# Filler products in TensorE's planned waits, k ahead of q, and another table of urgencies in a one-core decoder layer

## The reference

```python
# 1: causal self-attention, rotated before a second projection
q, k, v = rope(x @ wq.T), rope(x @ wk.T), x @ wv.T   # v is rotated too
qh, kh, vh = q @ wqi.T + bqi, k @ wki.T + bki, v @ wvi.T + bvi
x = layernorm(x + softmax(causal(qh @ kh.T / sqrt(8))) @ vh @ out_w.T + out_b)
# 2: cross-attention to the context, rotary on q and k
x = layernorm(x + attention(rope(x @ Wq.T + bq), rope(ctx @ Wk.T + bk), ctx @ Wv.T + bv) @ Wo.T + bo)
# 3: mixture of experts, the two best of eight by x @ wg.T
x = layernorm(x + sum_e weight_e * ((silu(x @ w1[e].T) * (x @ w3[e].T)) @ w2[e].T))
```

## Time and profile before

| | us |
|---|---|
| Median of 3 runs (259.11 to 260.6) | 259.66 |
| The profiled execution, its time | 258.49 |
| Its span, first to last instruction | 256.7 |

### The profile page before, as it was taken

One profiled execution on the slowest core, in us unless ns is written; L12 is line 12 of the kernel. 1 busy time (PEld: TensorE's weight loads), 2 busy tenths in 40 slices (PEclk: granted clock), 3 DMA queues, 4 the chain that ended last, 5 costly groups with the idle time before them and its releaser, 6 DMA issues. The chain is left out here.

```text
span 256.7 us, 4503 instructions
## 1 busy us (share of the span) xinstructions
PE 233.5 (91%) x1385; PEld 161.8 (63%) x1385; DVE 183.8 (72%) x616; ACT 158.4 (62%) x315; POOL 93.9 (37%) x151
## 2 busy tenths in 40 slices
PE   7679899999999999999998886999799998999980
PEld 3247556677665765586554365655378896898870
DVE  6558987888999697784847468694166884189855
ACT  1677857687898866886787642456656666122140
POOL 9993436165416164332535501065000100730100
PEclk9988999999999999999999997699999999999997
DMA  6980000011000400000221100001401111110101
GB/s 240 339 291 0 4 0 1 0 51 35 3 0 0 166 1 0 4 0 0 77 87 44 43 1 0 0 33 52 127 28 43 42 43 31 43 38 3 42 1 41
DMA packets 10567, 12.55 MB, mean 49 GB/s; under 512 B 1200, under 2 KB 7728, under 8 KB 10416
## 3 DMA queue, kind: packets, MB, share of 16 engines
q1 hardware_dynamic: 9456, 10.43, 12.6%
q0 software_dynamic: 512, 1.05, 1.4%
q10 hardware_dynamic: 576, 0.79, 0.9%
HBM read 9.25 MB, written 3.01 MB: 48 GB/s over the span
## 5 line engine op out<-in xcount | busy, mean ns | idle before, releaser
L1500 DVE CUSTOM_DVE_ANT_0 junk<-psA,c 128x128 bf16<-128x128 f32 (+3 forms) x128 | 55.9, 487 | 10.2 <-PE psA L1002 9.7
L1286 ACT ACTIVATE prob<-psB 128x512 f32<-128x512 f32 (+1 forms) x88 | 47.6, 560 | 14.6 <-PE psB L1031 11.6
L1031 PE MATMUL psB<-qb,kst 128*128 128x512 f32 (+3 forms) x128 | 38.6, 345 | 0.9 <-ACT prob L1286 0.6
L1002 PE MATMUL psA<-kst,qa 128*128 128x512 f32 (+1 forms) x88 | 36.8, 436 | 1.8 <-ACT kst L1249 1.4
L1505 DVE TENSOR_REDUCE negm<-psA 128x3 f32<-128x462 f32 (+1 forms) x48 | 26.0, 577 | 9.6 <-PE psA L1002 9.3
L1031 PEld LDWEIGHTS psB<-qb,kst 128*128 128x128 f32 x128 | 22.8, 188 | 14.8 <-ACT prob L1286 5.7
L1286 ACT ACTIVATE prob_more<-psB 128x512 f32<-128x512 f32 (+1 forms) x48 | 25.0, 527 | 7.8 <-PE psB L1031 7.4
L854 POOL TENSOR_SCALAR_AFFINE_SELECT prob<-prob 128x256 f32<-128x256 f32 x32 | 13.1, 408 | 40.2 <-ACT prob_more L1286 40.1
L1328 ACT ACTIVATE silu<-psA 128x512 f32<-128x512 f32 x16 | 9.5, 597 | 24.1 <-DVE hid L1661 14.2
L1002 PEld LDWEIGHTS psA<-kst,qa 128*128 128x128 f32 x88 | 16.8, 194 | 9.8 <-issue 6.0
L1002 PE MATMUL psA<-kc,qa 128*128 128x462 f32 (+2 forms) x64 | 19.3, 358 | 1.9 <-DVE negm L1505 1.9
(11 more groups left out here) (190 smaller groups left out, 541.9 us busy)
## 6 DMA issues: line engine op xcount, KB each, us to landing
c<-w_dram SPq DMA_DIRECT2D x8, 256.0 KB, 2.6
w<-w_dram SPq DMA_DIRECT2D x1, 1024.0 KB, 4.7
xs_dram<-kst SPq DMA_DIRECT2D x1, 960.0 KB, 7.2
ys_dram<-ys SPq DMA_DIRECT2D x7, 128.0 KB, 1.8
rest<-xs_dram SPq DMA_DIRECT2D x3, 256.0 KB, 2.7
c<-c_dram SPq DMA_DIRECT2D x1, 666.0 KB, 8.5
xT<-xt_dram SPq DMA_DIRECT2D x2, 256.0 KB, 4.8
x_tok<-x_dram SPq DMA_DIRECT2D x1, 512.0 KB, 10.0
```

The lines of the kernel that those rows point to most:

```text
L1002: last = nc.tensor.matmul(ps[:, c:c + heads * width].rearrange("p (n w) -> p n w", n=heads), qa[:, u % SLOTS, 128 * i:128 * i + 128], keys ...
L1031: last = nc.tensor.matmul(ps[:, c:c + S - 128 * kt], keys, qb[:, u % 2, 128 * kt:S], start=m == 0, stop=m == len(blocks) - 1, skip_group_c ...
L1286: nc.scalar.activation(dst, psB[n % SIZE["B"]][:, 0:cols], ACT.Exp, scale=SCALE).then_inc(b_done[n % SIZE["B"]], 1)
L1500: last = nc.vector.tensor_tensor_reduce(out=junk[:, p, cols], in0=psA[p][:, cols], in1=c32[:, C_MASK + S - width:C_MASK + S], scale=-1.0, ...
```

## The change

Three things change together.

- k takes the first place of q in each batch: U, H and the parts go k, q, v. PART and the buffer numbers derived from it follow, and so do the bias columns.
- A function `fillers()` goes over the planned order of PE in two stretches: from the second item to the first B of unit 0, and from the last B of units before 12 to the first B of unit 12 (cross-attention of batch 1). Where an item that ends after 6 us is planned to begin over 0.45 us after the end of the one before it, PE makes int((gap - 0.15) / 0.14) products ahead of it whose result nobody reads: in the first stretch zeros by 320 columns of the warm-up tile into psO; in the second, constants of c16 by 256 columns into the bank of psB that the next B will overwrite.
- The table EARLY is replaced as a whole.

```diff
-ROPE = {(b, w): "DVE" if (b, w) in ((0, "q"), (0, "k")) else "POOL" for b in range(B) for w in "qkv"}
+ROPE = {(b, w): "DVE" if (b, w) in ((0, "q"), (0, "k")) else "POOL" for b in range(B) for w in "kqv"}
...
-PART = {("q", 0): 0, ("k", 0): 1, ("q", 1): 2, ("k", 1): 3, ("c",): 4, ("x", 0): 5, ("x", 1): 6}
+PART = {("k", 0): 0, ("q", 0): 1, ("k", 1): 2, ("q", 1): 3, ("c",): 4, ("x", 0): 5, ("x", 1): 6}
...
-        for n, w in enumerate("qkv"):
+        for n, w in enumerate("kqv"):
...
-                before = (("H", (m // 3, "qk"[m % 3])) if m % 3 < 2 else ("VH", (m // 3,)), 0)
+                before = (("H", (m // 3, "kq"[m % 3])) if m % 3 < 2 else ("VH", (m // 3,)), 0)
...
-                deps.append((("H", (0, "k")), 0))
+                deps.append((("H", (0, "q")), 0))
...
-        for w in "qk":
+        for w in "kq":
...
 EARLY = {
-    ('A', 11): -36, ('A', 14): -9, ('A', 3): 80, ('A', 5): -7, ('A', 8): 65, ('A', 9): -52, ('B', 0): -26, ('B', 10): 139,
-    ('B', 11): 8, ('B', 12): 6, ('B', 5): 107, ('CV',): -8, ('F1', 1): -10, ('F1', 14): -29, ('F2', 0): -16, ('F2', 4): -9,
-    ('F3', 1): -3, ('F3', 9): -15, ('LN', 2, 0): -44, ('MP', 9): 13, ('MT', 1): -63, ('MT', 2): 28, ('MT', 4): -30,
-    ('MT', 9): -75, ('ONT', 0, 1): -45, ('OP', 0, 0): -52, ('OP', 0, 1): 67, ('OP', 1, 1): -73, ('OT', 7): -57,
...
-    ('SQ', 0, 1, 0): -24, ('SQ', 1, 0, 0): -27, ('U', 1, 'k'): -28, ('U', 1, 'v'): -42, ('VH', 0): 27, ('XS', 3): -75,
+    ('A', 10): -26, ('A', 11): -53, ('A', 15): -4, ('A', 3): -3, ('A', 6): -4, ('A', 7): -46, ('A', 8): 52, ('A', 9): -104,
+    ('B', 0): -81, ('B', 11): -22, ('B', 12): 4, ('B', 5): 133, ('CK',): 18, ('F1', 14): -50, ('F2', 0): -7, ('F2', 4): -31,
+    ('F3', 1): -12, ('F3', 3): -10, ('F3', 7): -3, ('F3', 9): -28, ('LN', 2, 0): -69, ('MP', 13): 18, ('MT', 11): -17,
+    ('MT', 2): 41, ('MT', 9): -115, ('ONT', 0, 0): -16, ('ONT', 0, 1): -65, ('OP', 0, 0): -44, ('OT', 2): -33,
+    ('OT', 7): -99, ('PV', 1): -51, ('PV', 12): -75, ('PV', 8): -22, ('PV', 9): -12, ('R1', 3): -2, ('R1', 4): -19,
...
+    ('SK', 1, 0): -11, ('SQ', 0, 0, 1): -25, ('SQ', 0, 1, 2): 11, ('U', 1, 'q'): -39, ('U', 1, 'v'): -64, ('XS', 1): 9,
 }
...
+def fillers():
+
+    table = tasks()
+    order = ORDER["PE"]
+    first, last = order.index(("B", (0, 0))), order.index(("B", (B * NG + NG, 0)))
+    hole = max(n for n, item in enumerate(order) if item[0] == "B" and item[1][0] < B * NG + NG and n < last)
+    counts = {}
+    for n in [*range(1, first), *range(hole + 1, last)]:
+        item, before = order[n], order[n - 1]
+        if item == before:
+            continue
+        gap = ENDS[item, 0] - table[item][0][0][1] - ENDS[before, 0]
+
+        if ENDS[item, 0] > 6 and gap > 0.45:
+            counts[item] = int((gap - 0.15) / 0.14)
+    return counts
+
+
+FILLERS = fillers()
...
-            for item in ORDER["PE"]:
+            for n_item, item in enumerate(ORDER["PE"]):
                 kind, args = item
+                if item in FILLERS:
+                    ahead = [other for other in ORDER["PE"][n_item:] if other[0] == "B"][0]
+                    ps = psO
+                    if ahead[1][0]:
+
+                        loaded(s_c16, 16)
+                        ps = ring_bank("B", ahead)
+                    for _ in range(FILLERS[item]):
+                        if ahead[1][0]:
+                            nc.tensor.matmul(ps[:, 0:256], c16[:, 0:128], c16[:, 0:256], start=True, stop=True)
+                        else:
+                            nc.tensor.matmul(ps[:, 0:320], warm[:, 384:512], warm[:, 0:320], start=True, stop=True)
...
-    bcol = [ib[0:D], ib[D:2 * D], bq, bq[swap4], bk, bk[swap4]]
+    bcol = [ib[D:2 * D], ib[0:D], bq, bq[swap4], bk, bk[swap4]]
```

More of the change, by code:

```diff
@@ L709, in parts_made @@
                 b, w = divmod(n, 2)
-                job_done(eng, "H", b, "qk"[w])
+                job_done(eng, "H", b, "kq"[w])
             else:
@@ L817, in _ @@
                     b, w = args
-                    n = 3 * b + "qkv".index(w)
+                    n = 3 * b + "kqv".index(w)
                     m = ROPED.index(item)
@@ L821, in _ @@
                     before = n - 2
-                    job_filled(pool, ("H", (before // 3, "qk"[before % 3])) if before % 3 < 2 else ("VH", (before // 3,)))
+                    job_filled(pool, ("H", (before // 3, "kq"[before % 3])) if before % 3 < 2 else ("VH", (before // 3,)))
                     if m == 0:
@@ L940, in _ @@
                     b, w = args
-                    n = 3 * b + (w == "k")
+                    n = 3 * b + (w == "q")
                     ps = bank(JOB[item])
@@ L1402, in _ @@
                         m = n - 2
-                        job_filled(dve, ("H", (m // 3, "qk"[m % 3])) if m % 3 < 2 else ("VH", (m // 3,)))
+                        job_filled(dve, ("H", (m // 3, "kq"[m % 3])) if m % 3 < 2 else ("VH", (m // 3,)))
                     dve.wait_ge(s_ca, 16)
```

## The result

| us | before | after |
|---|---|---|
| Median of 4 runs each (range) | 259.58 (259.11 to 260.6) | 256.69 (256.36 to 257.5) |
| The profiled execution, its time | 258.49 | 257.5 |
| Its span | 256.7 | 255.8 |
| Its mean granted clock | 0.973 | 0.994 |

The kernel after takes 0.989 of the time of the kernel before, with a 95% interval of 0.985 to 0.993: 2.9 us less. Every median, ratio and interval in this document is taken from the executions within 1.5% of the fastest of the same kernel on the chip; the number in brackets is theirs, with the number made behind "of" where it is larger. The profiled execution of before was the shortest of its four and that of after the longest of its four, so the two traces differ by 1.0 us only.

A forecast was written before the change was run, and what follows sets the result against it. PE was taken to bound the dense stages, DVE 16.6 to 29.8 us, with two slow-clock stretches. Terms -1.2 - 0.3 - 2.3 + 0.3 = -3.5 us took the profiled 258.49 to 255.0; plus 1.17, forecast 256.2 us, range 252.7 to 259.8.

The forecast's parts named there:

- part 3: Slow stretch from 157.6 us: fillers keep PE at 2.4 GHz, bringing POOL's first scatter 2.3 us earlier.
- 1. k ahead of q: Head: with k first, kst is done at 14.1 us and scores A start at 14.8, 1.2 us earlier.
- ACT is free for kst: Head: ACT, done with the second high part at about 12.0 us, makes kst, which is done at 14.1.
- Rival (b): Head: the rotation of v holds back the gain of k first, 0.65 instead of 1.2 us: 256.8 us; chance 0.08.
- 2. The early stretch: Head, about 18 to 21 us: removing the slow clock gives only 0.3 us, since DVE is nearly full there.
- 4. The fillers: Head and hole: filler products match the real waits in sum but not place by place, costing 0.3 us.
- 5. Order and table: Every queue's order may differ after the table exchange; taken as 0 us, with ends -1.5 and +2.5.
- one burst in the way: Dense stages: an in-order PE stall behind one burst, such as the out-projection, would cost 1.05 us.
- Rival (c): Out-projection of batch 1, OP(0, 1), at 134.12 us comes later and lengthens the hole: 262.2 us; chance 0.12.
- (d): New order also squeezes 1.5 us from the dense stages, and the later slow stretch gives 1 more: 253.7 us; chance 0.12.
- Rival (a): Head and hole: fillers miss the real waits or the clock falls later where none stands: 258.8 us; chance 0.20.
- sign of being wrong: Anywhere in the kernel: a granted clock of 0.50 for 3 us or more would show the forecast wrong.

The follow-up runs named there:

- table a: Kernel after with another table of urgencies from a random search, items of the hole ordered as in the kernel before: 253.07 us, 0.9805 of before.
- table b: Kernel after with a second table of urgencies from the same search, keeping the new order in the hole: 254.15 us, 0.984 of before.

## Why the prediction was right, and where it wasn't

The forecast was 256.2 us and the median is 256.69, with the sign, the clock and part 3 as told. But that the sum is met so closely is luck: the first term was too large, one of 1.76 us was missing, and the medians moved 1.9 us more than the two traces. The profiled execution was to become 255.0 us and took 257.5, the scatter was to come 3.5 us earlier and came 0.65, and with 12 executions each the change of 3.5 us measured 1.1 on chip P and 1.6 on R. Point by point:

**1. k ahead of q: the mechanism right, the size off.** The scores were to start at 14.8 us, 1.2 earlier. Where the first products ran as quickly as before, they started at 14.96 and 15.06: 0.9 to 1.0. The step that failed is "ACT is free for kst ..., where DVE starts on the low part". In the timeline of the head of after DVE takes its share of kst first, and the low part of q, its select and qa all wait for it:

```profile
4.43 3.30 PE L968 MATMUL psJ<-xT,wa 128*128 128x512 f32 x4 [0.22 <-DMA xT<-xt_dram]
...
12.38 1.67 PE L960 MATMUL psO<-warm 128*128 128x320 bf16 x11
12.58 0.76 DVE L1455 TENSOR_SCALAR kst<-psJ,c 32x512 fp32r<-32x512 f32 x1 [1.00 <-PE psJ L931]
...
13.37 0.75 DVE L1443 SCALAR_TENSOR_TENSOR low<-psJ,bcol,high 128x512 fp32r<-128x512 f32 x1
14.38 0.47 PE L930 MATMUL psJ<-high,fr 128*128 128x512 f32 x1 [0.33 <-DVE low L1443]
...
15.12 0.60 ACT L1271 ACTIVATE qa<-psJ 128x512 fp32r<-128x512 f32 x1 [0.43 <-PE psJ L931]
...
15.77 0.50 PE L1032 MATMUL psA<-kst,qa 128*128 128x512 f32 x1
```

qa is what comes last now, not kst. The first line hides the gain in after's own trace: the first projection took 3.30 us here and 1.98 in the kernel without fillers, and everything behind it starts about 0.8 us later. At XT(0, 1) 0.3 to 0.6 us is left (140.88 to 141.15 against 141.48), and the new table has a part in that: the prediction kept the whole 1.2 with the remark that DVE is full from there on. Rival (b) fell: the new order moves v's projection back, so that POOL ends the rotation at 24.82 us instead of 21.59; the product that reads it follows at 24.96, and PE is busy until then.

**2. The early stretch: -0.3 us predicted, some 0.2 by one pair of traces.** In the order before, the trace on R with hole fillers has no dip in the head and takes 125.29 us from A (16.03) to XT(0, 1); the first trace of before has one and takes 125.51 from an A at nearly the same time (15.97). So the small size fits. In the new order the traces with a dip also start A 0.6 to 0.8 us earlier, and no run took the dip away alone.

**3. The stretch at 157.6 us: -2.3 us predicted, -2.1 to -2.3 measured.** From XT(1, 0) to the scatter nine of the ten traces with fillers in the hole took 8.43 to 8.46 us (table a 8.13), against 10.56 and 10.75 in the two of before; without a change of order it was -2.32. Against the new order without fillers (9.31) it is only 0.87. The router product took 1.00 to 1.03 us as a group instead of 1.81. In the order before DVE then waits only 0.21 us for it ahead of its search, so DVE came next as worked out; in the new order it still waits 0.69.

**4. The fillers: +0.3 us.** The price of one was right. In sum they cost nothing that shows: in the hole none in either order, in the head none in the new order. In the order before, for which the prediction counted them, those of the head cost 0.77 us, and the clock fell there in spite of them.

**5. Order and table: 0 us, and this was the mis-sized term.** In the hole the new order loses 1.76 us with fillers and 2.02 without (17.94 against 15.92). Counted from XT(0, 1), it adds up in three steps. Before, a product B stands ahead of both products PV, and then come OT and OP(1, 0):

```profile
144.22 0.79 PE L1027 MATMUL psB<-qb,kt_sb 128*128 128x512 f32 x1
144.94 1.06 PE L1054 MATMUL psO<-prob,vc_sb 128*32 128x512 f32 x8
145.93 1.12 PE L1059 MATMUL psO<-prob,vblk 128*128 128x512 f32 x2
...
147.84 0.63 PE L1069 MATMUL psJ<-c,po_sb 128*128 128x128 f32 x4 [0.78 <-ACT po_sb L1292]
...
150.94 1.13 PE L1084 MATMUL psJ<-wx,ot_sb 128*128 128x128 f32 x8
```

After, that B comes between the two PV:

```profile
144.42 1.07 PE L1084 MATMUL psO<-prob,vc_sb 128*32 128x512 f32 x8
145.41 0.49 PE L1057 MATMUL psB<-qb,kt_sb 128*128 128x512 f32 x1
145.75 0.72 PE L958 MATMUL psB<-c 128*128 128x256 bf16 x5
146.60 1.12 PE L1089 MATMUL psO<-prob,vblk 128*128 128x512 f32 x2
```

The first step is here: ACT's exponential of this B is later, and the second PV, which reads it, starts 5.41 us after XT(0, 1) instead of 4.45. The kernel without fillers has 5.41 too, with 0.69 us of waiting for that exponential where the five fillers stand. That is 0.96 us. The second step is small: OT(5) now stands behind the select SQ(1, 1, 0) as well and OP(1, 0) behind more score products, so OP(1, 0) starts 10.95 us after XT(0, 1) (at 152.14) instead of 9.46, 1.49 late. The norm passes this on unchanged: its last step on DVE begins at 157.34 instead of 156.14, 1.49 late as well. The third step is at the end: x_tok is complete at 158.44, but MT(12) and the product B(12, 0) at 158.53 stand ahead of XT(1, 0), and B waits 0.42 us for ACT's qb, so XT(1, 0) starts 0.43 us behind x_tok instead of 0.14. That is the other 0.3. These steps are read from the traces; none was put back by itself. Table a, which puts back the order of all items in the hole, has 4.45 and the old 15.92 us, and table b, which keeps the new one, 5.42 and 17.68: so it is the order and not the fillers. The prediction named "one burst in the way" (1.05 us) as a price but gave it to the dense stages and not to the hole, the one place where it lies on the path. The plan told it beforehand: it has XT(1, 0) 1.2 us later than before, and its end 0.2 us later. Rival (c) fell: OP(0, 1) runs at 133.8 us, 0.3 earlier. So did (d): PE's idle time from 29.8 to 138 us went from 1.72 only to 1.54 us.

**Where the gain then came from.** The sum by the measured terms is -0.3 (XT(0, 1)) + 1.8 - 2.1 - 0.3 (behind the scatter) - 0.1 (around the span) = -1.0 us: exactly the two profiled executions. The other 1.9 us of the medians is that this trace of before lies at the low end of its own executions and that of after at the high end; the first projection, 1.99 us in the one and 3.30 in the other, starts A some 0.8 us later, of which 0.04 to 0.3 us is left at XT(0, 1) (141.19 against 141.15 and 140.88). The rest isn't accounted for.

The many executions of before on Q and R tell what the change is worth. Of the 34 that are counted, 26 had a mean clock of 0.973 to 0.981 and took 258.25 to 259.7 us, with a median of 258.9; eight had 0.990 to 0.994 and took 255.77 to 257.39, with a median of 256.3. The 12 made besides have the lower clock too (up to 260.76 us), so it is 38 of 46. With fillers in the hole and nothing else the kernel had 0.990 to 0.997 in all of 25, and took 256.33. So when the clock stays up, the kernel before is as quick as either; it falls in five of six executions and costs some 2.6 us there. The fillers in the hole insure against that. None of the eight was profiled: that it is the stretch behind the hole that stays up in them is inferred from the mean clock and the time. The other parts, k first, the table and the head's fillers, together cost 0.7 us beside the hole's fillers alone (chip R); without any fillers they give nothing (chip P). The prediction read the dips as a fixed part of one trace, and took over the offset of 1.17 us between it and the median without asking what is in it.

Rival (a) was half right, at another place: on chip P the clock fell between 178 and 192 us, in waits where no filler stands, and in one trace on R at 182 us. That is also what the prediction set as a sign of being wrong, 0.50 for 3 us or more, which the first chip doesn't show. The change gave 1.1 us on P, 1.6 on R and 2.9 on the first chip.

What stays open: what the "remote" wait of ACT is, why only chip P has it, what holds the late fillers ahead of XS(1), and how much of the loss in the hole comes through to the end: at the scatter the whole change is 1.6 us behind the hole's fillers alone on R, in the medians 0.7.

## What to carry to other kernels

Where the granted clock falls behind a stretch of short waits on the path of the end, cheap products in these waits can hold it; put them there alone, price them per place by the waits of the trace, and leave the stages where another engine is the bound. Look in the trace whether the wait comes behind the fillers or ahead of them: ahead, they are added to it. Time such a change over many executions, since here it took away the executions in which the clock falls rather than a fixed cost. And when a table that orders the work is exchanged with it, compare the order of the few items ahead of the critical stretch, above all of the products whose results a slower engine must turn round before PE can go on: here it gave back 1.8 of the 2.1 us, and a table that kept the old order there, and did better ahead of it, won 4.0 us more, 5.5 below the kernel before.

## What the runs showed of the hardware

- The clock fell at the end of the hole though PE stood still for no more than 1.46 us at a time. The Trainium skill ("TensorE: Matmul & The Clock Gate", A second HAM failure mode) tells of a kernel whose clock goes up and down with short stops alone; this trace agrees.
- The same four projection products at the start took 1.98 to 3.46 us from execution to execution, with a recorded clock of 1.00 each time; nothing in the record of the clock tells them apart. Under the same record of 1.00 ten zero products of 320 columns took 0.28 us each at 1.36 us, and eleven of the same shape 0.15 each at 12.38. The same page of the Trainium skill (Seeing it yourself) calls the recorded events unreliable: in the head the trace agrees. At 158 to 164 us it doesn't: there a recorded 0.50 and a router product of twice the time go together, and the record went to 1.00 with a gain of the size worked out from it.
- 20 fillers more, in later waits, cost 0.78 us; 25 in the hole cost nothing. In the hole what is left of PE's waits comes behind the fillers (0.36 and 0.43 us at the two largest), ahead of XS(1) it came before them (0.78).
